# Cross attention with its loop over batches written out on all engines, and the mask column read from the whole table

## The chip, the cores and the metric
The kernel runs on one NeuronCore of a Trainium2 chip. A core has five engines, each with its own instruction stream: TensorE (PE in the profile, with PEld for its weight loads), VectorE (DVE), ScalarE (ACT), GpSimd (POOL) and SyncE (SP), which here issues the transfers. They are kept in step by semaphores. The metric is the device time of one execution in microseconds (us), as the median of several.

## The reference
A model block on 8 batches of 128 query tokens: cross attention over a context of 2048 tokens per batch, a self attention with three branches, and two feed-forward parts, one of them with experts. The change touches only the cross attention. Its core, from the reference:
```python
        sim = jnp.where(mask[:, None, None, :], sim, max_neg)
        sim = jnp.clip(sim, -5.0, 5.0)
```
Here `sim` are the scores q k^T * DH ** (-0.5) of 16 heads of 64, and the mask (8 x 2048) says which context tokens of a batch count. The softmax of `sim` then weighs the values; keys and values are projections of the context by a 512 x 2048 matrix. The kernel clips the raw scores, ahead of the factor 1/8, so at plus and minus 40 (`RAW_CLIP`): a masked token gets -40 as its upper bound in place of +40.

## The kernel before, in words
The stages run one behind the other, each a block in which all five engines have a stream of their own, with a barrier between two blocks. `stage_cross` is the second stage. It runs from about 100 to 2092 us.

A batch is 64 steps (`SL`). A step takes one tile of 128 context tokens for 4 heads, and a step's work passes from engine to engine in a software pipeline:
- TensorE multiplies for the scores of step s (`ps_s`, L723), for the weighted values of step s - 3 (`ps_o`, L684), and for one unit of the projection of keys or values of the next context block (`ps_p`, L673, 12 matmuls of 512 columns). The scores of step s wait for the clip of step s - 1, since both use the same `ps_s`.
- ScalarE copies the projection (L522) and the right half of the scores (`right`, L568), takes the exponential twice (L555, L559), and rounds the context (`c_hi`, L576).
- VectorE subtracts for the low part of keys or values (L600), adds the two halves of the scores (L640), clips them between the mask's bound and -40 (`sc`, L644), and subtracts for the low part of the exponentials (`e_hl`, L653). Four times a batch it also closes a group of heads: L614, the reciprocal L619, and `O_sb = U * REC` (`o_sb`, L626). The last runs at steps 2, 6, 34 and 38 of a batch.
- GpSimd sums the exponentials (`es`, L483) and makes the low part of the context (`c_lo`).
- SyncE issues the transfers: context blocks (L383), the stacked keys (`k_hl`, L396), queries (L388), outputs (L409).

The mask stands as the table `top`, 128 x 128: 16 columns for each batch. VectorE copies the 16 columns of the batch to `topi` at step 0, and the clip reads one column of `topi` as its upper bound, one number per partition.

TensorE's stream is written out for all 8 batches. The other four have the first batch written out, batches 1 to 6 as one body in a hardware loop (`eng.Fori`, L367), whose semaphore values and addresses are computed in registers, and the last batch written out:
```python
        def over_batches(eng, body):
            body(0, True, False)
            with eng.Fori(1, B - 1) as i:
                body(i, False, False)
            body(B - 1, False, True)
```
The loop so turns five times. In later stages there are other such loops, of few instructions on these engines, that turn once each: L1024 on all engines (159 instructions on VectorE, 206 on ScalarE), L1986 on ScalarE, L2115 on VectorE, L2198 on TensorE.

Of the kernel before, what the change touches and what calls it, by code (L numbers as in the profile page):

```python
# [29 lines left out]
P = 128  # L30
B = 8
# [3 lines left out]
M = 2048  # L35
# [6 lines left out]
GRP = 4  # L42
# [5 lines left out]
RAW_CLIP = CLIP * DH ** 0.5  # L48
# [228 lines left out]
def stage_cross(nc, ctx_t, mask, q_hi_d, q_lo_d, o_t, WKV, C, RAW, wo, OT):  # L277
# [4 lines left out]
    with ExitStack() as ctx:  # L282
        sb = lambda n, s, d=F32: ctx.enter_context(nc.sbuf_tensor(n, s, d))
        sem = lambda n: ctx.enter_context(nc.semaphore(n))
# [5 lines left out]
        SC = sb("sc", [P, 2, 512])  # L290
# [12 lines left out]
        O_sb = sb("o_sb", [P, 2, P])  # L303
        mask_u8 = sb("mask_u8", [P, P], U8)
        top = sb("top", [P, P])
        topi = sb("topi", [P, M // P])
        ps_s = ctx.enter_context(nc.psum_tensor("ps_s", [P, 2, 512], F32))
        ps_p = ctx.enter_context(nc.psum_tensor("ps_p", [P, 2, 512], F32))
        ps_o = ctx.enter_context(nc.psum_tensor("ps_o", [P, GRP, 512], F32))
# [2 lines left out]
        q_in = [sem("q_in0"), sem("q_in1")]  # L312
        ones_raw_set, ones_set = sem("ones_raw_set"), sem("ones_set")
        right_out, halves_added, k_in = sem("right_out"), sem("halves_added"), [sem("k_in0"), sem("k_in1")]
        top_done, topi_done = sem("top_done"), sem("topi_done")
        chi_done, clo_done = sem("chi_done"), sem("clo_done")
        proj_done, p_free, kv_hi = sem("proj_done"), sem("p_free"), sem("kv_hi")
        scored, clipped, exp_hi, expd, e_lo = sem("scored"), sem("clipped"), sem("exp_hi"), sem("expd"), sem("e_lo_done")
# [22 lines left out]
        def after(s, by):  # L341

            return [(2 * hf + GL - 4 * (L + by >= SL)) for L, hf, GL in ENDS if (L + by) % SL == s]

        def has_kv(s, last):
            return not (last and s >= SL - BS + NEXT)
# [4 lines left out]
        def unit_at(i, s):  # L351

            return i * SL + NA + s
# [7 lines left out]
        def k_landed(i, blk, n):  # L361

            return 64 * (2 * (i * SLB + blk) + n // 2 + 1)

        def over_batches(eng, body):
            body(0, True, False)
            with eng.Fori(1, B - 1) as i:  # L367
                body(i, False, False)
            body(B - 1, False, True)

        TAIL = range(SL, SL + 8)
        WO_AT = {50: 0, 53: 1, 56: 2, 59: 3}
# [3 lines left out]
        @block.sync  # L376
        def _(sp):
            sp.dma_start(mask_u8[:], mask).then_inc(mask_in, 16)

            def load(i, m):  # L380

                at = i * (M // BLK) + (m // SLB) * (M // BLK) + m % (M // BLK)
                sp.dma_start(RAW[:, m % 2], ctx_t[bass.ds(at, 1)].rearrange("o p k f -> (o p) k f")).then_inc(raw_in[m % 2], 16)  # L383

            def queries(i, hf):
                for e, src in enumerate((q_hi_d, q_lo_d)):
                    for r in range(2):
                        sp.dma_start(Q2[r * DH:(r + 1) * DH, hf, :, e * P:(e + 1) * P].bitcast(F32),  # L388
                                     src[HP * hf:HP * hf + HP, :, bass.ds(i * P, P)].rearrange("c (h p) t -> p (c h) t", h=2)
                                     ).then_inc(q_in[hf], 16)  # L390

            def stack(n):

                for hh in range(2):
                    for e in range(2):
                        sp.dma_start(K2[e * DH:(e + 1) * DH, n, hh, :].bitcast(F32), KS[hh * DH:(hh + 1) * DH, n % 2, e, :]  # L396
                                     ).then_inc(k_in[n % 2], 16)
            queries(0, 0)
            for u, (kind, n) in enumerate(AHEAD):
                if kind == K:  # L400
                    sp.wait_ge(p_free, u + 1)
                    stack(n)
            load(0, 2)
            load(0, 3)
            queries(0, 1)

            def store(i, hf, GL):
                sp.wait_ge(o_done, 4 * i + 2 * hf + GL + 1)
                sp.dma_start(o_t[bass.ds(i, 1), HP * hf + 2 * GL:HP * hf + 2 * GL + 2].rearrange("o c p t -> p (o c) t"), O_sb[:]  # L409
                             ).then_inc(o_out, 16)  # L410

            def body(i, first, last):
                for s in range(SL):
                    S = i * SL + s
                    if s % BS == 0:
                        m = s // BS + 3
                        if not (last and m >= SLB) and not (first and m < 4):
                            sp.wait_ge(clo_done, KC * (i * SLB + m - 3))
                            load(i, m)
                    if s % BS == 0 and (s or not first):  # L420
                        sp.wait_ge(clipped, S)
                        stack(2)
                        stack(3)
                    if s % BS in (KT, KT + 1) and has_kv(s - 1, last):
                        sp.wait_ge(p_free, unit_at(i, s - 1) + 1)
                        stack(s % BS - KT)
                    if s == 1 and not first:
                        sp.wait_ge(scored, i * SL)
                        queries(i, 1)
                    if s == SL // 2 and not last:  # L430
                        sp.wait_ge(scored, S)
                        queries(i + 1, 0)
                    if last and s == WO_LOAD:
                        sp.wait_ge(clo_done, KC * (B * SLB - 2))
                        for j in range(4):
                            sp.dma_start(quarter(WO_raw, j).rearrange("p (k f) -> p k f", k=2), wo.rearrange("(k p) n -> p k n", p=P)[:, 2 * j:2 * j + 2]
                                         ).then_inc(wo_in[j], 16)
                    if last and s == OT_LOAD:
                        sp.wait_ge(o_out, 16 * 4 * 2)
                        for n in range(2):  # L440
                            sp.wait_ge(k_in[n], k_landed(B - 1, SLB - 1, 2 + n))
                        for b in range(2):
                            sp.dma_start(OT[:, b], o_t[b].rearrange("c p t -> p c t")).then_inc(ot_in, 16)
                    for n in after(s, 7):
                        if n >= 0 or not first:
                            store(i - (n < 0), n % 4 // 2, n % 2)
            over_batches(sp, body)
            for GL in range(2):
                store(B - 1, 1, GL)
            sp.wait_ge(o_out, 16 * 4 * B)  # L450
            sp.wait_ge(ot_in, 32)

        @block.gpsimd
        def _(g):
# [29 lines left out]
            def body(i, first, last):  # L484
                for s in range(SL):
# [10 lines left out]
                        g.wait_ge(wo_hi, j + 1)  # L496
                        g.tensor_tensor(quarter(WO_lo, j), quarter(WO_raw, j), quarter(WO_hi, j).bitcast(F32), ALU.subtract).then_inc(wo_lo, 1)
                    group_steps(i, s, first)
            over_batches(g, body)
            for s in TAIL:  # L500
                if s == SL:
                    sums(B, -1, False)
# [2 lines left out]
        halves = ps_s[:].rearrange("p b (j e q) -> p (b j) e q", j=2, e=2)  # L505
# [11 lines left out]
        def _(a):  # L517
# [43 lines left out]
            def body(i, first, last):  # L561
                for s in range(SL):
# [18 lines left out]
                        a.wait_ge(wo_in[j], 16)  # L581
                        a.copy(quarter(WO_hi, j), quarter(WO_raw, j)).then_inc(wo_hi, 1)
                    group_steps(i, s, first)
            over_batches(a, body)
            for s in TAIL:
                if s == SL:
                    exps(B, -1, False)
# [3 lines left out]
        def _(v):  # L591
# [6 lines left out]
            def evac_lo(kv, u, kind, n):  # L598
                v.wait_ge(kv_hi, kv + 1)
                v.tensor_tensor(kv_slice(False, kind, n), ps_view(u, kind), kv_slice(True, kind, n).bitcast(F32),  # L600
                                ALU.subtract).then_inc(p_free, 1)
# [26 lines left out]
            def body(i, first, last):  # L628
                for s in range(SL):
                    S = i * SL + s  # L630
                    if s == 0:
                        if not first:
                            v.wait_ge(clipped, S)
                        v.tensor_copy(topi[:], top[:, bass.ds(i * (M // P), M // P)]).then_inc(topi_done, 1)
                        v.wait_ge(topi_done, i + 1)
                    if s and has_kv(s - 1, last) or s == 0 and not first:
                        evac_lo(unit_at(i, s - 1), unit_at(0, s - 1), *unit_of((s - 1) % SL)[:2])
                    kt16 = place(s)[1] * KT + s % KT
                    v.wait_ge(right_out, S + 1)
                    v.tensor_tensor(halves[:, :, 0, :], halves[:, :, 0, :], RIGHT[:], ALU.add).then_inc(halves_added, 1)  # L640
                    if not (first and s < 2):
                        v.wait_ge(expd, S - 1)
                    v.wait_ge(halves_added, S + 1)
                    v.tensor_scalar(SC[:, s % 2].rearrange("p (j q) -> p j q", j=GRP), halves[:, :, 0, :], topi[:, kt16:kt16 + 1], -RAW_CLIP,  # L644
                                    ALU.min, ALU.max).then_inc(clipped, 1)
                    if s or not first:
                        exp_lo(i, s - 1)
                    group_steps(i, s, first)

            def exp_lo(i, s):  # L650
# [1 line left out]
                v.wait_ge(expd, i * SL + s + 1)  # L652
                v.tensor_tensor(E2[:, s % 2, :, 1, :], E[:, s % 2].rearrange("p (j q) -> p j q", j=GRP),  # L653
                                E2[:, s % 2, :, 0, :].bitcast(F32), ALU.subtract).then_inc(e_lo, 1)
            over_batches(v, body)
            for s in TAIL:
                if s == SL:
                    exp_lo(B, -1)
# [1702 lines left out]
```

## Time and profile before

| | |
|---|---|
| median of 3 runs | 3442.03 us (3441.99 to 3443.89) |
| the profiled execution | 3442.43 us, of which the span is 3440.6 us |
| mean granted clock of TensorE | 0.969 of 2.4 GHz |
| busy share of TensorE, VectorE, ScalarE, GpSimd | 93%, 72%, 50%, 51% |
| executed instructions in the trace | 53292 |

The span runs from the first to the last instruction of the program. A busy share is an average over all stages. A matmul's end is modelled, so what counts on TensorE is the distance from one to the next. A "q" behind an engine's name means its sequencer: branches, register arithmetic and the issue of transfers, which don't count as busy.

### The profile page before, as it was taken

How to read it: one execution, taken by the hardware profiler on the slowest of the kernel's cores; microseconds unless marked ns; L12 is line 12 of the kernel's file. 1: busy time of each engine (PE TensorE's matmuls, PEld its weight loads, DVE VectorE, ACT ScalarE, POOL GpSimd, SP SyncE). 2: the span in 40 equal slices, each digit the busy share in tenths (PEclk: the TensorE clock that was granted, in tenths of full speed). 3: DMA queues.
4: the chain of work that ended last, by engine and by line, in shares of the span. 5: the costliest groups of instructions: out<-in, count | busy, mean ns of one | idle time of the engine just before them, and what ended most of it. 6: DMA issues, size and time to landing. Idle time of an engine off the chain costs nothing. (4 is left out here: it accounts for less than half of the span.)

```text
span 3440.6 us, 53292 instructions
## 1 busy us (share of the span) xinstructions
PE 3202.8 (93%) x18116; PEld 2721.6 (79%) x18116; DVE 2479.6 (72%) x3443; ACT 1714.1 (50%) x3267; POOL 1746.9 (51%) x1124
## 2 busy tenths in 40 slices
PE   5999999999999999999999997988989887899996
PEld 4788888888888888887888886867777665678996
DVE  4699998898998998998999996676574744532213
ACT  3466666666666666666666662253353406221000
POOL 4365666565655565555556664051341427246573
PEclk9999999999999999999999998999999999899998
DMA  5554454444344444444454443100000110123230
GB/s 190 153 125 106 120 125 103 111 119 119 91 124 113 112 117 110 108 118 104 109 126 120 106 112 116 38 27 27 2 15 1 62 55 1 52 75 118 84 90 32
DMA packets 216129, 312.90 MB, mean 91 GB/s; under 512 B 28576, under 2 KB 122016, under 8 KB 207648
## 3 DMA queue, kind: packets, MB, share of 16 engines
q1 hardware_dynamic: 213024, 300.84, 33.7%
q0 software_dynamic: 2816, 8.46, 0.7%
q8 instruction: 151, 2.47, 0.3%
q14 instruction: 138, 1.13, 0.1%
HBM read 151.85 MB, written 23.13 MB: 51 GB/s over the span
## 5 line engine op out<-in xcount | busy, mean ns | idle before, releaser
L483 POOL TENSOR_TENSOR es<-es,e 128x512 f32<-128x512 f32 x480 | 622.1, 1296 | 744.5 <-ACT e L559 744.5
L653 DVE TENSOR_TENSOR e_hl<-e,e_hl 128x512 fp32r<-128x512 f32 x512 | 676.9, 1322 | 0.3 <-ACT e L559 0.3
L644 DVE TENSOR_SCALAR sc<-ps_s,topi 128x512 f32<-128x512 f32 x512 | 384.6, 751 | 72.0 <-issue 17.2
L492 POOL TENSOR_TENSOR c_lo<-raw,c_hi 128x512 fp32r<-128x512 f32 x248 | 427.5, 1724 | 0.0
L723 PEld LDWEIGHTS ps_s<-q_hl,k_hl 128*128 128x128 f32 x2048 | 310.7, 191 | 94.9 <-issue 55.6
L723 PE MATMUL ps_s<-q_hl,k_hl 128*128 128x256 f32 x2048 | 333.4, 286 | 42.7 <-DVE sc L644 42.2
L640 DVE TENSOR_TENSOR ps_s<-ps_s,right 128x512 f32<-128x512 f32 x512 | 353.5, 690 | 13.2 <-ACT right L568 11.8
L673 PE MATMUL ps_p<-wa,c_hi 128*128 128x512 f32 x1024 | 343.5, 397 | 0.0
L673 PE MATMUL ps_p<-c_hi,wa 128*128 128x512 f32 x1024 | 339.1, 392 | 4.5 <-PEq L115 4.5
L684 PE MATMUL ps_o<-e_hl,v_hl 128*128 128x256 f32 x2048 | 334.1, 286 | 2.9 <-DVE e_hl L653 2.9
L568 ACT COPY right<-ps_s 128x512 f32<-128x512 f32 x512 | 303.2, 592 | 60.5 <-PE ps_s L723 60.2
L555 ACT ACTIVATE e_hl<-sc 128x512 fp32r<-128x512 f32 x512 | 325.2, 635 | 3.6 <-PE ps_o L684 2.6
L522 ACT CAST v_hl<-ps_p 128x512 fp32r<-128x512 f32 x256 | 150.2, 587 | 338.1 <-PE ps_p L673 337.7
L559 ACT ACTIVATE e<-sc 128x512 f32<-128x512 f32 x512 | 316.8, 619 | 0.0
L684 PEld LDWEIGHTS ps_o<-e_hl,v_hl 128*128 128x128 f32 x2048 | 287.1, 195 | 3.4 <-DVE e_hl L653 3.4
L522 ACT CAST ot<-ps_p 128x512 fp32r<-128x512 f32 x256 | 150.3, 587 | 279.8 <-PE ps_p L673 275.2
L1071 POOL TENSOR_TENSOR s<-s,a_mx 128x1536 f32<-128x1536 f32 x32 | 88.1, 2752 | 332.7 <-DVE a_mx L1222 332.7
L673 PEld LDWEIGHTS ps_p<-c_hi,wa 128*128 128x128 f32 x1024 | 194.0, 189 | 43.1 <-issue 4.9
L673 PEld LDWEIGHTS ps_p<-wa,c_hi 128*128 128x128 f32 x1024 | 197.0, 192 | 39.1
L600 DVE TENSOR_TENSOR ot<-ps_p,ot 128x512 fp32r<-128x512 f32 x256 | 175.9, 687 | 60.2 <-ACT ot L522 59.7
L600 DVE TENSOR_TENSOR v_hl<-ps_p,v_hl 128x512 fp32r<-128x512 f32 x256 | 176.1, 688 | 54.4 <-ACT v_hl L522 53.4
L673 PE MATMUL ps_p<-wa,c_lo 128*128 128x512 f32 x512 | 203.7, 398 | 0.0
(394 smaller groups left out, 7476.6 us busy)
## 6 DMA issues: line engine op xcount, KB each, us to landing
k_hl<-ot SPq DMA_DIRECT2D x1024, 128.0 KB, 2.9
raw<-in_ctx_t SPq DMA_DIRECT2D x64, 1024.0 KB, 6.4
raw<-in_L_ffn_W_experts SPq DMA_DIRECT2D x64, 256.0 KB, 3.0
q_hl<-q_hi_scratch SPq DMA_DIRECT2D x32, 256.0 KB, 5.6
q_hl<-q_lo_scratch SPq DMA_DIRECT2D x32, 256.0 KB, 6.4
raw<-in_L_xattn_Wkv SPq DMA_DIRECT2D x8, 512.0 KB, 4.8
q_hi_scratch<-qa_qh SPq DMA_DIRECT2D x16, 256.0 KB, 2.6
q_lo_scratch<-qa_ql SPq DMA_DIRECT2D x16, 256.0 KB, 3.8
```

What stands on the lines that cost most here:

```text
L483: g.tensor_tensor(ES[:, GL], ES[:, GL], e, ALU.add).then_inc(summed, 1)
L492: g.tensor_tensor(C_lo[:, n % 2, k, :], RAW[:, n % 2, k, :], C_hi[:, n % 2, k, :].bitcast(F32), ALU.subtract).then_inc(clo_done, 1)
L555: a.activation(E2[:, s % 2, :, 0, :], sc, ACT.Exp, scale=DH ** -0.5).then_inc(exp_hi, 1)
L559: a.activation(E[:, s % 2], SC[:, s % 2], ACT.Exp, scale=DH ** -0.5).then_inc(expd, 1)
L568: a.copy(RIGHT[:], halves[:, :, 1, :]).then_inc(right_out, 1)
L600: v.tensor_tensor(kv_slice(False, kind, n), ps_view(u, kind), kv_slice(True, kind, n).bitcast(F32), ALU.subtract).then_inc(p_free, 1)
L640: v.tensor_tensor(halves[:, :, 0, :], halves[:, :, 0, :], RIGHT[:], ALU.add).then_inc(halves_added, 1)
L644: v.tensor_scalar(SC[:, s % 2].rearrange("p (j q) -> p j q", j=GRP), halves[:, :, 0, :], topi[:, kt16:kt16 + 1], -RAW_CLIP, ALU.min, ALU.m ...
L653: v.tensor_tensor(E2[:, s % 2, :, 1, :], E[:, s % 2].rearrange("p (j q) -> p j q", j=GRP), E2[:, s % 2, :, 0, :].bitcast(F32), ALU.subtrac ...
L673: mm = t.matmul(ps_p[:, par % 2, :], lhs, rhs, start=m == 0, stop=m == 3 * KC - 1)
L684: mm = t.matmul(ps_o[:, 2 * GL + j // 2, (j % 2) * 256:(j % 2 + 1) * 256], V2[:, kt, GRP * GL + j, :], E2[:, s % 2, j].rearrange("p e q -> ...
L723: mm = t.matmul(ps_s[:, j // 2, (j % 2) * 256:(j % 2 + 1) * 256], K2[:, 2 * GL + j // 2, j % 2, kt * P:(kt + 1) * P], Q2[:, hf, GRP * GL + ...
```

## The change
The loop is gone: all 8 batches are written out on the four engines as they are on TensorE. `topi`, its copy and its semaphore are gone, and the clip reads its column straight from `top`. In all bodies `i` is now a number known at build time in place of a register.
```diff
-        topi = sb("topi", [P, M // P])
-        top_done, topi_done = sem("top_done"), sem("topi_done")
+        top_done = sem("top_done")
-        def over_batches(eng, body):
-            body(0, True, False)
-            with eng.Fori(1, B - 1) as i:
-                body(i, False, False)
-            body(B - 1, False, True)
+        def over_batches(body):
+            for i in range(B):
+                body(i, i == 0, i == B - 1)
...
-            over_batches(sp, body)
+            over_batches(body)
...
             def body(i, first, last):
                 for s in range(SL):
                     S = i * SL + s
-                    if s == 0:
-                        if not first:
-                            v.wait_ge(clipped, S)
-                        v.tensor_copy(topi[:], top[:, bass.ds(i * (M // P), M // P)]).then_inc(topi_done, 1)
-                        v.wait_ge(topi_done, i + 1)
...
-                    v.tensor_scalar(SC[:, s % 2].rearrange("p (j q) -> p j q", j=GRP), halves[:, :, 0, :], topi[:, kt16:kt16 + 1], -RAW_CLIP,
+                    v.tensor_scalar(SC[:, s % 2].rearrange("p (j q) -> p j q", j=GRP), halves[:, :, 0, :], top[:, i * (M // P) + kt16:i * (M // P) + kt16 + 1], -RAW_CLIP,
                                     ALU.min, ALU.max).then_inc(clipped, 1)
```
How many instructions the stage has on each engine, counted in the compiled programs (waits and register arithmetic included, a transfer as one):

| engine | before: first batch, loop body, last batch | together | after |
|---|---|---|---|
| VectorE | 342, 428, 353 | 1123 | 2753 |
| ScalarE | 475, 558, 483 | 1516 | 3860 |
| GpSimd | 169, 273, 170 | 612 | 1345 |
| SyncE | 162, 197, 144 | 503 | 1192 |
| TensorE | written out | 11130 | 11130 |

A batch in the middle that is written out has so 343 instructions on VectorE, 484 on ScalarE, 168 on GpSimd and 148 on SyncE, 1143 together.

VectorE before, at the end of the loop's body and what stands behind it. The row of L367 is the turn; what follows it in the list is the last batch, but at a turn the stream goes back to the body's start, which reads like the next fence:
```order
L653 TENSOR_TENSOR e_hl<-e,e_hl 128x4x128
L609 ISA
L614 TENSOR_TENSOR u<-ps_o,t 64x256 x2
L367 REGISTER_ALU
L367 COMPARE_AND_BRANCH
L634 COPY topi<-top 128x16
L600 TENSOR_TENSOR v_hl<-ps_p,v_hl 128x8x64
```
VectorE before, at the entry to the loop, behind the first batch, with the start of the body:
```order
L614 TENSOR_TENSOR u<-ps_o,t 64x256 x2
L367 UNCONDITIONAL_BRANCH
L367 ISA
L634 ISA
L634 COPY topi<-top 128x16
L635 REGISTER_ALU
L599 REGISTER_ALU
L600 TENSOR_TENSOR v_hl<-ps_p,v_hl 128x8x64
L639 REGISTER_ALU
L640 TENSOR_TENSOR ps_s<-ps_s,right 128x4x128
L642 REGISTER_ALU
L644 TENSOR_SCALAR sc<-ps_s,topi 128x512
```
VectorE after, at the change from batch 1 to 2 (its lines have moved up: L611 is the former L614, L597 the former L600, L632, L636 and L645 the former L640, L644 and L653):
```order
L611 TENSOR_TENSOR u<-ps_o,t 64x256 x2
L597 TENSOR_TENSOR v_hl<-ps_p,v_hl 128x8x64
L632 TENSOR_TENSOR ps_s<-ps_s,right 128x4x128
L636 TENSOR_SCALAR sc<-ps_s,top 128x512
L645 TENSOR_TENSOR e_hl<-e,e_hl 128x4x128
L597 TENSOR_TENSOR v_hl<-ps_p,v_hl 128x8x64
```
The branch, the copy and the register arithmetic are gone from between the batches; the work itself stands in the same order.

## Rows read from the trace of the kernel before

**Rows 1.** The page: busy us, share of the span, executed instructions.
```profile
PE 3202.8 (93%) x18116; PEld 2721.6 (79%) x18116; DVE 2479.6 (72%) x3443; ACT 1714.1 (50%) x3267; POOL 1746.9 (51%) x1124
```
**Rows 2.** Windows: us; busy PE, PEld, DVE, ACT, POOL; clock, DMA share, GB/s.
```profile
261.39:382.45 121.06, 120.32 (x650) 103.49 (x649) 110.84 (x139) 81.67 (x156) 71.92 (x52) 1.00 0.47 116
...
503.14:631.19 128.05, 122.28 (x650) 105.38 (x649) 110.52 (x138) 81.35 (x155) 72.62 (x52) 0.97 0.45 110
631.19:751.88 120.69, 120.07 (x650) 103.42 (x649) 110.84 (x137) 81.53 (x155) 72.48 (x52) 1.00 0.48 116
...
1499.05:1627.99 128.94, 122.18 (x650) 105.33 (x649) 110.47 (x139) 81.36 (x155) 72.61 (x52) 0.97 0.44 109
...
1748.69:1869.31 120.62, 119.99 (x650) 103.33 (x649) 110.52 (x138) 81.41 (x154) 72.50 (x52) 1.00 0.47 116
1869.31:1989.96 120.65, 120.07 (x650) 103.44 (x649) 110.44 (x138) 81.88 (x156) 72.39 (x52) 1.00 0.43 107
sum 1728.57, PE 1692.74 PEld 1458.08 DVE 1549.96 ACT 1140.85 POOL 1014.88; mean PE 120.91 PEld 104.15 DVE 110.71 ACT 81.49 POOL 72.49
```
**Rows 3.** Timeline of VectorE at a turn: start, us, instruction, [idle before it <- releaser].
```profile
598.63 0.26 DVE L634 COPY topi<-top 128x16 f32 x1 [2.48 <-issue]
599.02 0.69 DVE L600 TENSOR_TENSOR v_hl<-ps_p,v_hl 128x512 fp32r<-128x512 f32 x1
599.63 0.69 DVE L640 TENSOR_TENSOR ps_s<-ps_s,right 128x512 f32<-128x512 f32 x1
603.51 0.75 DVE L644 TENSOR_SCALAR sc<-ps_s,topi 128x512 f32<-128x512 f32 x1 [3.19 <-issue]
```
**Rows 4.** Timeline of TensorE at the same turn.
```profile
604.40 1.20 PE L723 MATMUL ps_s<-q_hl,k_hl 128*128 128x256 f32 x4 [5.44 <-DVE sc L644]
```
**Rows 5.** Waits of TensorE, 261.39 to 1989.96: total us, times, longest.
```profile
PE ps_s L723 <- DVE sc L644: 35.3, 29, 6.4
```
**Rows 6.** Windows, behind the same turn (columns of rows 2).
```profile
603.00:610.00 7.00, 5.60 (x19) 4.83 (x20) 5.59 (x7) 1.74 (x3) 1.59 (x1) 0.55 1.14 231
```
**Rows 7.** Records of line L367, 580 to 600: duration ns, start us.
```profile
L367 SPq COMPARE_BRANCH  x1: 59/59/59, 587.6 to 587.6; - x1
L367 SPq FUSED_REGOPS  x1: 56/56/56, 587.9 to 587.9; - x1
...
L367 ACTq COMPARE_BRANCH  x1: 45/45/45, 592.5 to 592.5; - x1
...
L367 POOLq COMPARE_BRANCH  x1: 45/45/45, 594.0 to 594.0; - x1
L367 ACTq FUSED_REGOPS  x1: 50/50/50, 595.0 to 595.0; - x1
...
L367 DVEq COMPARE_BRANCH  x1: 72/72/72, 595.4 to 595.4; - x1
L367 POOLq FUSED_REGOPS  x1: 47/47/47, 596.6 to 596.6; - x1
L367 DVEq FUSED_REGOPS  x1: 58/58/58, 598.4 to 598.4; - x1
```
**Rows 8.** Timeline of VectorE at the change from batch 6 to 7.
```profile
1840.84 0.86 DVE L614 TENSOR_TENSOR u<-ps_o,t 64x256 f32<-64x256 f32 x2
1841.73 0.22 DVE L634 COPY topi<-top 128x16 f32<-128x16 f32 x1
1841.99 0.69 DVE L600 TENSOR_TENSOR v_hl<-ps_p,v_hl 128x512 fp32r<-128x512 f32 x1
```
**Rows 9.** DMA queue of instructions, 120 to 355 and then 608 to 844: packets, MB.
```profile
q14 instruction: 7, 0.06, 0.1%
q14 instruction: 11, 0.09, 0.1%
```
**Rows 10.** Records of line L1024, the turn of VectorE in a later stage.
```profile
L1024 DVEq COMPARE_BRANCH  x1: 80/80/80, 2456.9 to 2456.9; - x1
L1024 DVEq FUSED_REGOPS  x1: 70/70/70, 2457.2 to 2457.2; - x1
```

More of the change, by code:

```diff
@@ L498, in body @@
                     group_steps(i, s, first)
-            over_batches(g, body)
+            over_batches(body)
             for s in TAIL:
@@ L583, in body @@
                     group_steps(i, s, first)
-            over_batches(a, body)
+            over_batches(body)
             for s in TAIL:
@@ L654, in exp_lo @@
                                 E2[:, s % 2, :, 0, :].bitcast(F32), ALU.subtract).then_inc(e_lo, 1)
-            over_batches(v, body)
+            over_batches(body)
             for s in TAIL:
```

## Prediction
> **What bounds the kernel now.** The page first: TensorE is busy 93% of the span, VectorE 72% [rows 1]. A share over stages with different limits says little, so I cut the cross-attention stage into pieces that must be alike. The output multiply `O_sb = U * REC` runs at steps 2, 6, 34 and 38 of each batch's 64, so from its run at step 38 to that at step 6 of the next batch, and from step 6 to step 38, are 32 steps each, with the same work: each piece has its 650 matmuls [rows 2]. There are 14 such pieces between 261.39 and 1989.96 us. Those inside a batch take 120.69 us, with TensorE busy 120.07 of them at a granted clock of 1.00. So inside a batch the stage is bound by the stream of TensorE, and an edit that only spares VectorE, ScalarE or GpSimd work there is worth nothing.
>
> The pieces that hold a change of batch fall into two kinds. Where the batch changes inside the hardware loop (batches 1 to 2, up to 5 to 6: five turns) a piece takes 128.05 us in the first case and 128.94 in the last, at a clock of 0.97. Where it changes from the loop to the code written out behind it (6 to 7) it takes 120.62, and at the entry to the loop (0 to 1) 121.06 [rows 2]. The same boundary is thus free in straight code and costs about 8 us at a turn of the loop.
>
> The timeline of VectorE at the turn at 595 us shows where. The copy to `topi` comes after 2.48 us of idle time, and three instructions on, the clip (`sc`, L644) comes after another 3.19 us; both are put down to "issue", that is to nothing that the profile shows as waited for [rows 3]. The next scores on TensorE (L723) need that clip: 5.44 us idle [rows 4]. Summed over the 14 pieces TensorE waits 35.3 us for the clip, and for nothing else [rows 5]. When it resumes, the granted clock is down: 0.55 over 603 to 610 us, that is mostly the 1.2 GHz level after the idle stretch, where it was at the 2.4 GHz level before [rows 6]. What the idle time does not explain of the 8 us is this second price.
>
> Is it the turn or the body? The records of L367 tell [rows 7]: VectorE's compare-and-branch starts at 595.4 us and the first instruction of the next pass at 598.4, 3.0 us later; ScalarE takes 2.5 and GpSimd 2.6, SyncE only 0.3. Bodies of 428, 558 and 273 instructions pay, the 197 of SyncE do not; and in a later stage the turn of VectorE's 159 instructions takes 0.3 us [rows 10]. In a window of batch 2 the instruction queue q14 brought 11 packets, in one as long of batch 0, in straight code, 7 [rows 9]. I read this as instructions fetched again at the turn. ScalarE's and GpSimd's own 2.5 us hide behind work queued before; VectorE's two stalls set the end.
>
> By the Trainium skill (Runtime: NRT & Kernel Launch, Instruction fetch mechanics) a taken branch to a page outside the loaded window stalls until that is fetched, and crossing pages in straight code is mostly hidden; the trace agrees with both, by the 3.0 us and the 120.62 us piece. The same page gives most engines room for 512 instructions, and read by size alone VectorE's 428 would fit and the turn be cheap. The row shows 3.0 us, so the row decides; by the other reading the sum would be near nothing for the fetch.
>
> **The change, part by part.**
> (1) Five turns go. They take 1627.99 - 503.14 = 1124.85 us less the four pieces between them, 4 x 120.69 = 482.76: 642.09 us. As straight code each should take what the boundary 6 to 7 takes, 120.62: 603.10. Gain 39.0 us. It contains both of VectorE's stalls, TensorE's slow clock and the settling after it.
> (2) The entry to the loop: 121.06 to 120.62, gain 0.4 us.
> (3) Register arithmetic in the body: a piece inside a batch takes 120.69 in the loop and 120.65 in batch 7 [rows 2]; for the six batches 6 x 0.04 = 0.2 us. TensorE covers it; without that cover it would be some 80 short instructions a pass.
> (4) The eight copies to `topi` with their two waits. In straight code the copy starts at 1841.73, VectorE takes up the next instruction at 1841.99 and had been done at 1841.70 [rows 8]: 0.3 us of VectorE each. At 6 to 7 the piece with the copy is no longer than its neighbours [rows 2], so TensorE hides it; worth 0 to 8 x 0.3 = 2.4 us, and I take 0. The clip now reads its column from `top` in place of `topi`, one number per partition either way: 0. The wait on `clipped` ahead of the copy goes with it; the overwriting that it guarded against no longer exists. What remains late at a boundary is what is late at 6 to 7.
> (5) Straight code is longer: VectorE 2753 instructions in the stage in place of 1123, ScalarE 3860 for 1516 (counted in the compiled programs, as all numbers of instructions here). The issued work is the same but for registers and branches. Cost of fetching in sequence: batches 0 and 7 already run so on all five engines, with no idle time to show for it in [rows 2]; I take 0, the upper end is the slower rival below.
> (6) No DMA is added or moved; SyncE issues the same ones from constants, and it is not what is waited for at the turn.
> (7) Later stages: same code, at other places in instruction memory. Their loops turn once each. Taken as 0, bounds below.
>
> Sum: 39.0 + 0.4 + 0.2 = 39.6 us. The profiled execution took 3442.43 us, with a span of 3440.6; 3442.43 - 39.6 = 3402.8. It lies 0.4 above the median of the three runs (3442.03), so that a median of 3402.4 would be as good.
>
> **Rivals.**
> A, the forecast: the turns go and nothing comes. 3399 to 3407, the width from part (4) on the one side, and on the other from a start and stage ends that shift by a few tenths to 4 us. Chance 0.84.
> B, later loops now pay. Behind the longer code the bodies of the later stages lie elsewhere, and one that did not have to be fetched again may have to. For it: the price at a turn, 7.4 to 8.3 us where it is on the path [rows 2]. Against: bodies below 273 instructions turned in 0.3 us [rows 7, 10], wherever they lay. One such turn gives 3410, three 3427. Chance 0.07.
> C, the gain is partial: the boundary in straight code is no better where it also reloads queries for the next batch with all transfers of SyncE, as at 0 to 1 and unlike 6 to 7. At 121.06 for each of the boundaries the gain shrinks by 6 x 0.44 = 2.6 us: 3405, inside A. Only with a stall left of VectorE's second kind, 3.19 us at each of five, and its clock, would it be 3420 to 3425. Chance 0.04.
> D, slower: straight code stalls on its own fetches. Batches 1 to 6 are now about 2058 instructions of VectorE (2753 less the 342 and 353 that were straight already). Seven packets for some 1143 instructions of four engines a batch [rows 9] is one in about 163, so 13 for VectorE. If each held it 3.19 us like the one in [rows 3], and TensorE lost 8/5.67 = 1.4 times that with the clock, the cost is 58 us: 3461. It decides from 39.6 / (13 x 1.4) = 2.2 us a packet on. Against it: batches 0 and 7 met such packets too and show none. Chance 0.03.
> E, nothing changes: the idle time put down to "issue" is not the turn's but comes at each 64th step wherever, or TensorE loses its clock when it runs 1900 us without a rest. The former is refuted by 6 to 7, against the latter stand only the pieces without a turn, at 1.00, at most four in a row. About 3442. Chance 0.02.
>
> **How the numbers follow.** Some 0.2% (7 us) is what a measurement of this kernel tells from no change. A, B and C are all faster by more; D is slower; E the same: 0.95, 0.02, 0.03. For the range A's 3399 to 3407 is widened a little on both sides, into the cheap end of B and C below, and for a full part (4) above part (3) on the fast side: 3397 to 3409.
>
> **What the profile after would show.** All 14 pieces between runs of `O_sb = U * REC` at 120.6 to 121.1 us; no "issue" idle time above 1 us before the clip; TensorE's wait for the clip down from 35.3 us to under 8; a granted clock of 1.00 from 261 us to the end of the last batch; the last run of `O_sb = U * REC` 39.6 us earlier, and the rest of the span as long as before. Wrong would be: pieces of 124 us or more (D or C), or a tail that has grown (B).

## The result, and the profile after

The changed kernel took 3406.74 us (median of 4 runs, 3397.42 to 3408.25), the kernel before 3442.01 us (median of 4, 3440.38 to 3443.89) beside it: 0.9898 of the time, with a 95% interval of 0.988 to 0.9916. The forecast was 3402.8 us, in a range of 3397 to 3409. The profiled execution of the changed kernel is the slowest of its four, 3408.25 us with a span of 3406.4; that of before had 3442.43 and 3440.6. So the two traces differ by 34.2 us in span, and the medians by 35.3, where 39.6 was forecast.

The page of the changed kernel, busy time of each engine and the two queues that bring instructions (packets, MB, share):
```profile
PE 3191.8 (94%) x18116; PEld 2712.8 (80%) x18116; DVE 2479.0 (73%) x3435; ACT 1717.7 (50%) x3267; POOL 1744.4 (51%) x1124
...
q8 instruction: 151, 2.47, 0.3%
q14 instruction: 95, 0.78, 0.1%
```
The second queue before:
```profile
q14 instruction: 138, 1.13, 0.1%
```
Beside [rows 1] VectorE ran 8 instructions fewer, the eight copies to `topi`, and TensorE is busy 11.0 us less for the same 18116 matmuls: it ran less of its work at the low clock. The queue q14 brought 95 packets, where it had brought 138 before, although the program is longer: the loop had fetched the same instructions again and again. The other, q8, brought 151 packets in both.

The pieces of [rows 2], cut at the same runs of `O_sb = U * REC`, for the changed kernel (us; busy PE, PEld, DVE, ACT, POOL; clock, DMA share, GB/s). Shown are the change from batch 0 to 1, that from 1 to 2, the last piece, and the sum of the 14:
```profile
264.46:385.09 120.63, 120.05 (x650) 103.41 (x649) 110.40 (x137) 81.77 (x156) 72.39 (x52) 1.00 0.47 116
...
505.71:626.33 120.62, 120.04 (x650) 103.38 (x649) 110.43 (x137) 81.78 (x156) 72.46 (x52) 1.00 0.48 116
...
1832.60:1953.44 120.84, 120.26 (x651) 103.59 (x650) 110.99 (x137) 81.96 (x156) 72.40 (x52) 1.00 0.42 107
...
sum 1688.98, PE 1680.90 PEld 1447.89 DVE 1550.39 ACT 1145.12 POOL 1013.65; mean PE 120.06 PEld 103.42 DVE 110.74 ACT 81.79 POOL 72.40
```
No piece stands out any more: 13 of them take 120.61 to 120.64 us, and the last 120.84. The sum is 1728.57 - 1688.98 = 39.59 us shorter. The clock is 1.00 in all of them.

VectorE at the change from batch 1 to 2:
```profile
597.85 0.87 DVE L611 TENSOR_TENSOR u<-ps_o,t 64x256 f32<-64x256 f32 x2
598.75 0.69 DVE L597 TENSOR_TENSOR v_hl<-ps_p,v_hl 128x512 fp32r<-128x512 f32 x1
599.35 0.69 DVE L632 TENSOR_TENSOR ps_s<-ps_s,right 128x512 f32<-128x512 f32 x1
600.15 0.75 DVE L636 TENSOR_SCALAR sc<-ps_s,top 128x512 f32<-128x512 f32 x1
600.82 1.18 DVE L645 TENSOR_TENSOR e_hl<-e,e_hl 128x512 fp32r<-128x512 f32 x1
```
Nothing is idle here. In [rows 3] this stretch held 2.48 us of "issue" ahead of the copy and 3.19 ahead of the clip. TensorE's wait for the clip, over the 14 pieces (us in total, times, longest):
```profile
PE ps_s L715 <- DVE sc L636: 8.1, 28, 0.3
```
It was 35.3 us with a longest of 6.4 [rows 5]; what is left are 28 waits of 0.3 us at most.

**Where the rest went.** The stages, cut at the first matmul of each, first of the kernel before: the projection of the queries, the cross attention, its output projection, and self-attention.
```profile
0.00:99.12 99.12, 57.13 (x224) 44.85 (x225) 40.91 (x86) 30.23 (x37) 37.66 (x17) 0.97 0.55 192
99.12:2097.34 1998.22, 1941.58 (x10369) 1671.57 (x10369) 1773.97 (x2187) 1306.44 (x2462) 1159.55 (x834) 0.98 0.46 113
2097.34:2177.74 80.40, 73.50 (x352) 63.17 (x353) 58.73 (x178) 14.25 (x17) 26.63 (x15) 0.96 0.42 125
2177.74:2723.69 545.95, 494.79 (x3218) 400.74 (x3218) 342.14 (x430) 232.88 (x465) 178.95 (x72) 0.95 0.05 17
```
And of the changed kernel:
```profile
0.00:102.09 102.09, 58.65 (x224) 45.96 (x225) 40.88 (x86) 30.09 (x37) 37.66 (x17) 0.96 0.54 186
102.09:2060.71 1958.62, 1928.81 (x10368) 1660.78 (x10368) 1774.33 (x2179) 1310.33 (x2462) 1157.83 (x834) 0.99 0.47 115
2060.71:2146.09 85.38, 76.49 (x353) 65.78 (x353) 57.70 (x178) 14.24 (x17) 26.62 (x15) 0.92 0.40 118
2146.09:2689.72 543.63, 492.27 (x3219) 399.46 (x3219) 342.02 (x431) 232.83 (x465) 178.95 (x72) 0.96 0.06 17
```
The cross attention is 39.60 us shorter. The queries' stage took 2.97 us more, the output projection 4.98 more, self-attention 2.32 less, and what follows 0.23 less: 34.2 in all. The experiments tell in part which of these belong to the change.

### The profile page after: what moved, and what is told of

Its sections match the earlier page's. It is cut to its first block and busy times, and to the rows that moved or that the text cites. A ratio compares the mean times of both kernels' runs of the same rounds, so it can differ in the third digit from the quotient of the medians.

```text
span 3406.4 us, 51290 instructions
## 1 busy us (share of the span) xinstructions
PE 3191.8 (94%) x18116; PEld 2712.8 (80%) x18116; DVE 2479.0 (73%) x3435; ACT 1717.7 (50%) x3267; POOL 1744.4 (51%) x1124
## 3 DMA queue, kind: packets, MB, share of 16 engines
q8 instruction: 151, 2.47, 0.3%
## 5 line engine op out<-in xcount | busy, mean ns | idle before, releaser
L645 DVE TENSOR_TENSOR e_hl<-e,e_hl 128x512 fp32r<-128x512 f32 x512 | 680.0, 1328 | 0.3 <-ACT e L556 0.3
L636 DVE TENSOR_SCALAR sc<-ps_s,top 128x512 f32<-128x512 f32 x512 | 384.5, 751 | 55.7 <-ACT e L556 1.4
L632 DVE TENSOR_TENSOR ps_s<-ps_s,right 128x512 f32<-128x512 f32 x512 | 353.1, 690 | 8.9 <-ACT right L565 7.7
L597 DVE TENSOR_TENSOR ot<-ps_p,ot 128x512 fp32r<-128x512 f32 x256 | 175.6, 686 | 59.7 <-ACT ot L519 59.2
L597 DVE TENSOR_TENSOR v_hl<-ps_p,v_hl 128x512 fp32r<-128x512 f32 x256 | 175.5, 686 | 47.8 <-ACT v_hl L519 47.3
L665 PE MATMUL ps_p<-c_lo,wa 128*128 128x512 f32 x512 | 201.7, 394 | 0.0
```

Of the source, the lines that this page charges most:

```text
L665: mm = t.matmul(ps_p[:, par % 2, :], lhs, rhs, start=m == 0, stop=m == 3 * KC - 1)
```

## Experiments

Times are medians, and each ratio is against runs of the kernel before beside it; "14 pieces" is the sum of the windows of [rows 2] in the profiled execution. In these experiments the runs of one kernel lay 5 to 19 us apart (before: 3438.71 to 3454.24), so that the ratio settles the sign and about half a per cent, and the pieces settle the mechanism. The kernel before had a median of 3448.1 us beside e1 to e4, 3447.16 beside e5 to e7 and 3444.71 beside e8 to e10; so times that were expected from its 3442, as for e1 (3412.28 us, where 3400 to 3410 were expected) and e3 (3427.17, for 3417 to 3421), came out some us longer, and the ratios are what to compare.

| kernel | runs, us | ratio (95%) | 14 pieces, us | pieces with a turn, us |
|---|---|---|---|---|
| before | | 1 | 1728.57 | 128.05 to 128.94 |
| changed | 3406.74 | 0.9898 (0.988 to 0.9916) | 1688.98 | none |
| e1 only VectorE written out | 3412.28 | 0.9902 (0.988 to 0.9924) | 1689.13 | 120.16 to 120.64 |
| e2 all but VectorE written out | 3447.03 | 0.9999 (0.9987 to 1.001) | 1729.30 | 128.00 to 129.02 |
| e3 two turns in place of five | 3427.17 | 0.9932 (0.9907 to 0.9958) | 1704.49 | 127.91, 128.19 |
| e4 written out, copy kept | 3408.63 | 0.9882 (0.9859 to 0.9905) | 1689.41 | none |
| e5 loop, no copy | 3429.05 | 0.9944 (0.9927 to 0.9962) | 1708.05 | 123.86 to 125.08 |
| e6_pad40 | 3424.53 | 0.9928 (0.9907 to 0.9949) | 1706.76 | 123.22 to 124.38 |
| e6_pad8 (one run) | 3454.8 | | 1733.20 | 128.84 to 130.61 |
| e7 changed again | 3409.86 | 0.988 (0.9859 to 0.9902) | 1688.83 | none |
| e8 e5 with 6 copies ahead | 3443.29 | 1.0 (0.9989 to 1.001) | 1728.21 | 127.96 to 128.78 |
| e9 before with 127 copies ahead | 3431.9 | 0.9964 (0.995 to 0.9978) | 1710.38 | 124.19 to 125.44 |
| e10 self-attention written out too | 3404.7 | 0.9887 (0.987 to 0.9903) | 1688.86 | none |

My theory was the prediction's: the price is VectorE's, at its turns, and nothing else in the change counts. The rivals: the price belongs to all engines together or to another one; it belongs to the copy and its waits; it belongs to the loop as such, not to its turns.

**e1, e2: whose turn is it?** In e1 only VectorE leaves the loop:
```
+        def written_out(eng, body):
+            for i in range(B):
+                body(i, i == 0, i == B - 1)
...
-            over_batches(v, body)
+            written_out(v, body)
```

> The kernel before, with only VectorE's loop written out; ScalarE, GpSimd and SyncE keep theirs, and the copy to topi stays. Theory (VectorE's two stalls at a turn set the end, the 2.5 us of ScalarE and GpSimd lie behind work queued before): nearly all of the gain, 36 to 40 us in the 14 pieces between runs of O_sb = U * REC, pieces with a turn 120.6 to 121.5 us, a time of 3400 to 3410. Rival (each engine's refetch costs, VectorE's only comes last): the next late engine takes over, pieces with a turn at 123 to 126 us, a time of 3415 to 3430.

In e2 SyncE, GpSimd and ScalarE leave it and VectorE stays.

> The kernel before, with the loops of ScalarE, GpSimd and SyncE written out and VectorE's kept. Theory: pieces with a turn stay at 128 to 129 us, the time within 3 us of 3442. Rival (the instruction queue is shared, so VectorE waits while the others fetch; or SyncE's turn makes the keys late): the pieces shrink by 1 to 4 us each, a time of 3422 to 3437.

A piece with a turn in e1, columns as above:
```profile
499.22:619.38 120.16, 119.83 (x650) 103.47 (x649) 110.08 (x139) 81.21 (x155) 72.08 (x52) 1.00 0.48 117
```
Records of e1 at its turn (duration ns, start us):
```profile
L367 ACTq COMPARE_BRANCH  x1: 45/45/45, 588.6 to 588.6; - x1
...
L367 POOLq COMPARE_BRANCH  x1: 45/45/45, 590.1 to 590.1; - x1
...
L367 ACTq FUSED_REGOPS  x1: 50/50/50, 591.2 to 591.2; - x1
...
L367 POOLq FUSED_REGOPS  x1: 47/47/47, 593.4 to 593.4; - x1
```
ScalarE and GpSimd still lose 2.6 and 3.3 us at the turn, and TensorE feels nothing of it (the 120.16 us are an output multiply 0.5 us early: the next piece has 121.12, and the 14 together are as long as in the changed kernel). The same piece of e2:
```profile
504.12:633.14 129.02, 122.01 (x650) 105.18 (x649) 110.85 (x138) 81.72 (x156) 72.44 (x52) 0.97 0.44 109
```
With VectorE alone in the loop the whole price is there: 1729.30 us against 1728.57. The price is VectorE's, all of it, which settles the first rival.

**e3: per turn, or per kernel?** The loop runs over batches 1 to 3, with two turns; 4 to 7 are written out.
```
-            with eng.Fori(1, B - 1) as i:
+            with eng.Fori(1, B // 2) as i:
...
-            body(B - 1, False, True)
+            for i in range(B // 2, B):
+                body(i, False, i == B - 1)
```

> The kernel before, with the loop over batches 1 to 3 only on all four engines and batches 4 to 7 written out: two turns in place of five. Theory (a price per turn of about 7.8 us): the pieces together 3 x 7.8 = 23.4 us shorter than before, a time of 3417 to 3421 plus what the rest of the kernel scatters. Rival (a price for being in a loop, or for its entry, whatever the number of turns): no shorter than before, or as short as without a loop.

The second turn of e3, then the change from batch 3 to 4, where its loop ends, and that from 4 to 5, in straight code:
```profile
752.00:880.19 128.19, 121.86 (x650) 105.05 (x649) 110.60 (x138) 81.34 (x155) 72.69 (x52) 0.97 0.46 110
...
1000.89:1121.51 120.62, 119.99 (x650) 103.34 (x649) 110.52 (x139) 81.43 (x155) 72.54 (x52) 1.00 0.48 116
...
1242.14:1362.79 120.65, 120.07 (x650) 103.41 (x649) 110.78 (x139) 81.81 (x156) 72.49 (x52) 1.00 0.48 116
...
sum 1704.49, PE 1684.23 PEld 1450.98 DVE 1549.89 ACT 1142.78 POOL 1014.86; mean PE 120.30 PEld 103.64 DVE 110.71 ACT 81.63 POOL 72.49
```
Two turns cost 1704.49 - 1688.98 = 15.51 us, 7.8 each; the five of the kernel before 39.59, 7.9 each, with the 0.4 us of the entry in both sums. The price is one per turn.

**e4, e5: is it the copy?** e4 writes the loop out on all engines and keeps the copy to `topi` with its waits.

> The changed kernel, with the copy to topi, its two waits and its semaphore kept. Theory (TensorE hides the copy in straight code): all 14 pieces 120.6 to 120.7 us, as in the changed kernel, and the same time within its scatter, 3397 to 3409. Rival (the copy and its waits cost 0.3 us at each change of batch): the 7 pieces with a change of batch at 120.9 or more, together 2 us longer.

Its pieces sum to 1689.41 us against 1688.98. The seven with a change of batch, and so with a copy, take 120.62 to 120.65 us, together 0.06 us more than in the changed kernel; the rest comes from one piece inside batch 2, of 121.08 us, without a copy. So the copies hide under TensorE as part (4) had it. e5 is the other half alone: the loops stay, the copy and its waits go.
```
-                        v.tensor_copy(topi[:], top[:, bass.ds(i * (M // P), M // P)]).then_inc(topi_done, 1)
...
-... topi[:, kt16:kt16 + 1], -RAW_CLIP,
+... top[:, bass.ds(i * (M // P) + kt16, 1)], -RAW_CLIP,
```

> The kernel before with its loops, and only the other half of the change: the clip reads its column from top at an address computed in a register, without topi, its copy and its waits. Theory (the price is the turn's): pieces with a turn stay at 127 to 129.5 us, a time within 5 us of the kernel before. Rival (the copy, with its wait for the clip ahead of it, is part of the price at a turn): pieces with a turn shorter by 0.5 us or more each; and if the register addresses cost on the path, the pieces inside a batch grow above 120.7 us.

This was a miss: 123.86 to 125.08 us for a piece with a turn, and 1708.05 in all, half of the whole gain. VectorE of e5 at the turn:
```profile
597.46 0.69 DVE L599 TENSOR_TENSOR v_hl<-ps_p,v_hl 128x512 fp32r<-128x512 f32 x1 [2.39 <-issue]
...
598.99 0.75 DVE L638 TENSOR_SCALAR sc<-ps_s,top 128x512 f32<-128x512 f32 x1 [0.23 <-DVE ps_s L634]
...
602.55 0.70 DVE L634 TENSOR_TENSOR ps_s<-ps_s,right 128x512 f32<-128x512 f32 x1 [1.61 <-issue]
```
The first stall is as before, but the second now stands behind the clip, where TensorE has its scores already. Either the copy and its waits caused the stall ahead of the clip, or two stalls belong to the turn at a fixed distance in the program and the missing instructions moved the clip to the near side of the second.

**e6, e8, e9: the copy or the place?** These three shift the loop in instruction memory and leave its work alone, with copies of one column that VectorE makes once, ahead of the first batch:
```
+        PAD = sb("pad", [P, 64])
...
             v.wait_ge(top_done, 1)
+            for n in range(40):
+                v.tensor_copy(PAD[:, n:n + 1], top[:, 0:1])
```

> The kernel before with 40 copies of one column (128x1) on VectorE ahead of its first batch: no work of the loop changes, but its body starts 40 instructions later in instruction memory. Theory (at a turn VectorE waits for the fetch of two blocks of instructions, and the second stall stands where a block ends, 11 instructions behind the body's start): the end of the block is now 40 instructions earlier, thus ahead of the body's start, and the next one, with blocks of 128, 99 instructions behind it, by when it is fetched. No idle time of 3 us before the first clip; pieces with a turn 123.5 to 126 us, a time 12 to 25 us below the kernel before. Rival (the second stall belongs to the clip: its register operand or its semaphore): it stays before the first clip, and the pieces stay at 128 to 129 us.

> As with 40, but 8 such copies, so that the end of a block stands 3 instructions behind the body's start in place of 11. Theory: the second stall of about 3 us moves ahead, to the copy to topi or the first subtraction behind it (L600), and the clip has none; pieces with a turn about as long as before, 127.5 to 129.5 us. Rival: the stall stays before the clip.

VectorE of e6_pad40 at the turn, with the copy to `topi` and then the clip:
```profile
594.49 0.21 DVE L637 COPY topi<-top 128x16 f32 x1 [2.56 <-issue]
...
596.23 0.75 DVE L647 TENSOR_SCALAR sc<-ps_s,topi 128x512 f32<-128x512 f32 x1
```
The copy and its waits are all there, and the clip runs 1.74 us after the copy starts, where it was 4.88 us in [rows 3]. The gain is e5's: 1706.76 us in the pieces. VectorE of e6_pad8:
```profile
598.49 0.24 DVE L637 COPY topi<-top 128x16 f32 x1 [2.50 <-issue]
603.92 0.69 DVE L603 TENSOR_TENSOR v_hl<-ps_p,v_hl 128x512 fp32r<-128x512 f32 x1 [5.19 <-issue]
...
605.33 0.75 DVE L647 TENSOR_SCALAR sc<-ps_s,topi 128x512 f32<-128x512 f32 x1
```
With the loop seven instructions further back the stall comes right behind the copy, is 5.19 us long, and the pieces are a little dearer than before. The place is as expected; that the stall would be of 3 us, and the pieces at most 129.5 us, was not (128.84 to 130.61). e8 is e5 with 6 such copies (5 instructions more, by the compiled program), which should bring the clip behind the edge again; e9 is the kernel before with 127 (126 more), for the period.

> The kernel that keeps its loops and reads the mask column straight from top, whose pieces with a turn took 123.9 to 125.1 us, with 6 copies of one column on VectorE ahead of the first batch: 5 instructions more in the program, so that the clip is again the first instruction of the block that is missing at a turn, as in the kernel before. Theory (what that kernel gained was the place of the block's end, behind the clip in place of ahead of it, not the copy to topi): 3 us of idle time ahead of the first clip, pieces with a turn back at 127.5 to 129.5 us, a time within 5 us of the kernel before. Rival (the copy and its wait were the price): pieces stay at 124 to 125 us.

> The kernel before, topi and loops kept, with 127 copies of one column on VectorE ahead of the first batch (126 instructions more in the program, 2 less than a block of 128 if that is what a block holds), so that the end of the block stands 13 or 14 instructions behind the body's start, just behind the clip. Theory: the clip no longer waits, the second stall of 1.5 to 3 us comes before a later instruction; pieces with a turn at 124 to 126 us, a time 10 to 22 us below the kernel before. Rival (blocks of another size than 128, or the copy's absence was what helped): pieces at 127.5 us or more.

VectorE of e8, without the copy to `topi`:
```profile
592.31 0.69 DVE L602 TENSOR_TENSOR v_hl<-ps_p,v_hl 128x512 fp32r<-128x512 f32 x1 [2.48 <-issue]
...
597.67 0.75 DVE L641 TENSOR_SCALAR sc<-ps_s,top 128x512 f32<-128x512 f32 x1 [4.06 <-issue]
```
Five instructions made once took e5's gain back: 1708.05 to 1728.21 us in the pieces, ratio 1.0 (0.9989 to 1.001). The stall is ahead of the clip without any copy to `topi`. And VectorE of e9:
```profile
602.71 0.75 DVE L647 TENSOR_SCALAR sc<-ps_s,topi 128x512 f32<-128x512 f32 x1
...
605.87 0.69 DVE L603 TENSOR_TENSOR v_hl<-ps_p,v_hl 128x512 fp32r<-128x512 f32 x1 [1.81 <-issue]
```
The packets show the fetching at the turn itself. From 595 to 607 us, the turn of [rows 3], q14 brought the kernel before
```profile
q14 instruction: 6, 0.05, 1.4%
```
and the changed kernel none in the same 12 us. Two of the six came between 601 and 603 us, just ahead of the clip that started at 603.51.

**e7, e10.** e7 is the changed kernel again.

> The changed kernel once more, for the part outside the cross attention. Theory (the 5.4 us that the profiled execution gave back in the query stage and in the output stage behind the cross attention are scatter of the clock and of transfers there): the 14 pieces at 1688.9 to 1689.5 us again, the stage before them and the one behind them of other lengths, within the 79 to 86 us that kernels with loops show too. Rival (longer code makes the stage behind it slower): that stage at 85 us again.

Its first three stages, cut as above:
```profile
0.00:100.49 100.49, 56.33 (x225) 44.35 (x225) 40.91 (x86) 30.22 (x37) 37.55 (x17) 0.96 0.55 189
100.49:2057.97 1957.48, 1928.31 (x10369) 1660.42 (x10369) 1774.01 (x2179) 1310.30 (x2462) 1159.47 (x834) 0.99 0.47 115
2057.97:2140.01 82.04, 74.34 (x352) 63.75 (x353) 57.66 (x178) 14.26 (x17) 26.71 (x15) 0.95 0.41 123
```
The same code has an output projection of 82.04 us here and 85.38 in the first trace, and a query stage of 100.49 in place of 102.09: the first of these speaks against the rival of longer code, which expected 85 again. e10 writes the rounds of the self-attention out as well:
```
-            body(0, True, False)
-            with eng.Fori(1, NR - 1) as g:
-                body(g, False, False)
-            body(NR - 1, False, True)
+            for g in range(NR):
+                body(g, g == 0, g == NR - 1)
```

> The changed kernel with the rounds of the self attention written out on all engines too (its loop turned once). Theory (a branch far back is paid wherever it is on the path: TensorE's own branch there takes 3.7 us, with 752 instructions in its body): that stage shorter by 3.7 us of waiting and some us of slow clock behind it, from the 543 to 548 us of the runs so far to 537 to 543, a time 3 to 8 us below the changed kernel. Rival (TensorE waits there for others anyway): no difference beyond the scatter of some 5 us.

That stage of e10, and then the same stage of e5, which has its loop:
```profile
2137.24:2676.99 539.75, 492.64 (x3218) 398.63 (x3218) 341.81 (x430) 232.81 (x465) 178.94 (x72) 0.96 0.05 17
```
```profile
2159.09:2699.21 540.12, 490.86 (x3219) 398.50 (x3219) 342.16 (x431) 232.75 (x465) 179.06 (x72) 0.96 0.06 17
```
It is 3.88 us shorter than in the changed kernel, but e5 reached nearly the same with the loop in place, and the twelve traces with this loop scatter from 540.12 to 548.17; the two ratios overlap (0.987 to 0.9903, and 0.988 to 0.9916). The expectation took TensorE to wait the 3.7 us of its branch. It does not: the matmuls issued ahead run on, and it is idle for 0.81 us at the turn in the changed kernel, 0.73 in the one before. (The 752 instructions given there for the body are too few as well: between the starts of the two passes in the kernel before lie 816 matmuls and 815 weight loads.) Whether that loop costs anything is left open. No kernel here is measurably faster than the changed one.

## Why the prediction came out as it did

**Part (1), five turns, 39.0 us, and part (2), the entry, 0.4: right.** The turns' pieces take 120.62 to 120.64 us and the entry's 120.63, a gain of 38.96 and 0.43 us; the 14 pieces lost 39.59 us, and the whole stage 39.60, against a sum of 39.6. Taking the boundary 6 to 7 of the kernel before as the price of straight code was what made the sum good: the difference from it held both of VectorE's stalls and the slow clock behind them without splitting them. That the sum is right to a hundredth is luck: part (3), put at 0.2 us, gave 0.4 in the six pieces inside batches 1 to 6, and the last piece happened to be 0.2 longer.

**Attribution to VectorE, and 2.5 us of ScalarE and GpSimd hidden: right**, by e1 and e2.

**Part (4), the copy at 0: right for straight code**, by e4 (0.06 us for seven copies with their waits).

**Parts (5) and (6), and rival D: straight code costs nothing to fetch.** VectorE's 2753 instructions stand in no piece above 120.84 us, at 1.00. The instructions were indeed fetched, 9 packets in the second window of [rows 9], where straight code in batch 0 had 7 and the loop 11, and nobody waited. Rival D had reckoned one packet for 163 instructions; it is one for 127, so 16 for VectorE in place of 13.

**Part (7) and rival B: no turn came to cost more.** Behind the changed code the self-attention's loop turns VectorE in 0.3 us, as in [rows 10]; TensorE's own turn there holds a branch of 3.6 us before and of 3.7 after, hidden but for 0.7 and 0.8 us of idle time (e10); and that stage is 2.32 us shorter.

**Rivals C and E** fell with the pieces: no boundary has a stall left, and TensorE ran 14 pieces in a row, 1689 us, at a clock of 1.00.

**The sum as a time: 5.4 us off in the profiled execution (3408.25 for 3402.8), 3.9 in the median.** It was made against the one execution of before, whose other stages I took to stay. The query stage ran 2.97 us longer and the output projection 4.98, the rest 2.55 less. The first has the same code in both kernels. In the changed kernel TensorE ran at a granted clock of 0.50 from 76.80 to 80.20 us, where it had 1.00 before, and over the kernels here that stage takes 93.8 to 102.1 us: scatter. The output projection takes 82.04 to 85.38 us in two traces of the changed kernel and 81.8 and 82.56 in e10 and e4, which are written out on all engines too; in the nine kernels that kept a loop on some engine it takes 78.9 to 83.1 (81.1 in the mean). So three of the four lie among the nine and 85.38 alone stands outside: that is scatter for the most part, and whether 1 us of it belongs to the longer code is left open. (The expectation of e7 has 79 to 86 us for kernels with loops; their traces show 83.1 at most.)

The expectation "the rest of the span as long as before" was the wrong one: the last run of `O_sb = U * REC` came at 2055.0 us, 36.6 earlier and not 39.6, because the start had shifted. The shifts outside the pieces add up to 5.4 us, more than the 4 that rival A allowed for: the profiled execution lies above A's 3407 and only inside the wider 3409. The median, 3406.74, lies inside A. Two of the signs were missed by little or for a reason that has nothing to do with the turns: the wait for the clip was to be under 8 us and is 8.1, and the clock, 1.00 in all pieces, is 0.91 between the last piece and the last `O_sb = U * REC` (1953.44 to 2055.00), where it had been 0.88 before.

**What I had not asked: why the second stall fell ahead of the clip.** I put the second stall down to the turn and did not ask why it fell just ahead of the clip. By e8 and e9 it fell there because an edge of 128 instructions stood there: in the kernel before the clip was the first instruction behind it. Its place and not its work made about half of the gain: with the edge elsewhere five turns cost 17.8 us (e6_pad40, 1706.76 - 1688.98), not 39.6.

The Trainium skill (Runtime: NRT & Kernel Launch, Instruction fetch mechanics) gives refills in blocks of 256 instructions. The shift by two under 126 more instructions in e9 goes with 128 and not with 256, so for VectorE the runs decide. The other queue does fit the 256. Its packets have 16.4 KB (2.47 MB in 151), and in the second window of [rows 9] it brought 10 to the kernel before, while TensorE's records there, matmuls, weight loads and sequencer's, are 2623: one packet for 262. That q8 is TensorE's is inferred: it brought 151 packets to each kernel that left TensorE's stream alone, and 148 to e10, which did not.

## What to carry to other kernels

Look at the turn of a hardware loop on every engine: when the body is long (273 instructions paid here, 159 did not), the first instruction of the next pass comes 2.5 to 3.3 us after the branch, and on VectorE the first one past the next edge some 5 us after that, put down to "issue". Here it cost only on the engine that the bound one waits for, and writing out that engine alone brought it all (e1). Before a small edit inside such a loop is credited or blamed, shift the loop by a few instructions that do nothing: here five of them cost 20 us, all that the edit that they were added to had gained.

## What the runs showed of the hardware

- **Two arrivals at a turn, not one.** In six kernels whose turn of VectorE I read (before, e5, e6_pad8, e6_pad40, e8, e9) the first work of the body came after 2.35 to 2.56 us of idle time, and in five of them the first instruction past the edge 5.1 to 5.5 us after the body's first: 598.42 to 603.51 in the kernel before, 592.20 to 597.67 in e8, 600.57 to 605.78 in e9. What runs out in between is idle time. In the kernel before both stalls came at all five turns, 12.0 us ahead of the copy and 17.2 ahead of the clip in all. In e6_pad40 no edge came in the first few instructions, and no second stall shows.
- **Stalls in the loop and not in straight code.** The changed kernel fetched 9 packets in 236 us, and no piece there is longer than 120.64 us.
- **The low clock behind a short wait was nearly a third of the gain.** Over the 14 pieces TensorE is busy 1692.74 us before and 1680.90 after, 11.8 us less for the same matmuls. Its idle time fell from 35.83 to 8.08 us (the pieces' length less its busy time), by 27.8, of which its wait for the clip gave 27.2 (35.3 to 8.1). Together that is the 39.6: 70% idle time, 30% work at the lower clock behind it, as in [rows 6].
- **A branch that takes 3.7 us need not stop its engine.** TensorE's own turn in self-attention holds it, and TensorE was idle for 0.81 us there: it had matmuls issued ahead.
